# A selective-scan decoder layer: VectorE, not GpSimd, multiplies dt with the convolved input, between its products and its scans

## What is computed

```
proj = einsum('blh,he->bel', x, W_in);  hidden, gate = split(proj, 2)
hidden = silu(conv1d(hidden) + conv_bias)            # E = 1024 channels, 512 time steps
dt, Bm, Cm = split(hidden.T @ W_x, [128, 16, 16])
dts = softplus(dt @ W_dt + b_dt)                     # 1024 channels
dA  = exp(dts[..., None] * A)                        # N = 16 states for each channel
dBu = dts[..., None] * Bm * hidden[..., None]
state = dA * state + dBu                             # over the 512 time steps
y = (einsum(state, Cm) + hidden * D) * silu(gate);   out = y @ W_out
```

## Time and profile before

| | before |
|---|---|
| median of 3 runs | 1163.89 us (1163.69 to 1163.9) |
| the profiled execution: its time, and its span from first to last instruction | 1165.72 us, 1163.9 us |
| busy: VectorE, ScalarE, GpSimd, TensorE (matrix products) | 1026.1, 759.5, 748.2, 830.5 us |
| mean granted clock of TensorE | 0.874 of full speed |
| the 32 step inputs on GpSimd (L480) | 57.6 us busy |
| the dBu products on VectorE (L761, without those from `wide`) | 344.9 us busy |

### The profile page before, as it was taken

One profiled execution on the slowest core, in us unless ns is written; L12 is line 12 of the kernel. 1 busy time (PEld: TensorE's weight loads), 2 busy tenths in 40 slices (PEclk: granted clock), 3 DMA queues, 4 the chain that ended last, 5 costly groups with the idle time before them and its releaser, 6 DMA issues.

```text
span 1163.9 us, 10065 instructions
## 1 busy us (share of the span) xinstructions
PE 830.5 (71%) x2708; PEld 327.9 (28%) x2718; DVE 1026.1 (88%) x781; ACT 759.5 (65%) x1164; POOL 748.2 (64%) x419
## 2 busy tenths in 40 slices
PE   7923387877349689987459698987459657567884
PEld 2311032332024234432114233432114223222331
DVE  2569999999989998999989998899998999999833
ACT  3345567776536777786737686787655776777546
POOL 1027666667757856687766866677767867787433
PEclk9976789998679899999769899999859878787997
DMA  5174344453983343453992444344793353234000
GB/s 179 38 182 116 78 110 114 116 140 84 226 225 82 96 104 91 104 136 82 233 257 64 100 102 106 92 122 108 197 248 73 77 141 81 70 88 134 9 0 37
DMA packets 66681, 135.01 MB, mean 116 GB/s; under 512 B 13120, under 2 KB 19392, under 8 KB 66624
## 3 DMA queue, kind: packets, MB, share of 16 engines
q1 hardware_dynamic: 65904, 134.28, 45.6%
q10 hardware_dynamic: 720, 0.08, 0.0%
HBM read 62.75 MB, written 4.46 MB: 58 GB/s over the span
## 4 chain that ended last, share of the span: by engine, by line
issue 35%; DVE 28%; PE 22%; DMA 6%; ACT 5%; POOL 2%; SPq 2%; DVEq 0%; POOLq 0%; ACTq 0%
DVE st L767 19%; PE dense L866 15%; DVE dBu L761 4%; PE dense L922 3%; DMA wide<-w_out 2%; DMA Bb<-bc_rows 2%; PE dense L899 2%; DVE x L726 1%; DVE hs L745 1%; POOL st L456 1%; PE dBu L876 1%; SPq L340 1%; DVE xsc L818 1%; DVE dense L850 1%; ACT squares L592 1%
## 5 line engine op out<-in xcount | busy, mean ns | idle before, releaser
L456 POOL TENSOR_TENSOR st<-st,Cb 128x1024 f32<-128x1024 f32 x250 | 584.5, 2360 | 279.3 <-DVE dBu L761 256.0
L767 DVE TENSOR_TENSOR_SCAN st<-dA,dBu 128x1024 f32<-128x1024 f32 x256 | 570.0, 2266 | 0.0
L568 ACT ACTIVATE dA<-rep,Aneg 128x511 f32<-128x511 f32 x512 | 329.3, 710 | 119.9 <-DVE st L767 110.7
L761 DVE TENSOR_TENSOR dBu<-rep,Bb 128x1024 f32<-128x1024 f32 x250 | 344.9, 1423 | 37.9 <-DMA rep<-steps 10.9
L866 PE MATMUL dense<-xTs,Win 128*128 128x512 f32 x512 | 239.1, 611 | 14.7 <-DMA xTs<-xT 7.8
L899 PE MATMUL dense<-st,sel 128*32 128x512 f32 x1024 | 134.2, 665 | 112.8 <-POOL st L456 112.8
L866 PE MATMUL dense<-wide,hs 128*128 128x512 f32 x256 | 123.4, 640 | 37.9 <-DMA wide<-w_out 37.1
L866 PEld LDWEIGHTS dense<-xTs,Win 128*128 128x128 f32 x512 | 98.3, 196 | 147.2 <-issue 146.5
L922 PE MATMUL dense<-pj,Win 128*128 128x512 f32 (+1 forms) x192 | 94.5, 638 | 32.4 <-issue 22.2
L480 POOL TENSOR_TENSOR steps<-steps,hs 128x512 f32<-128x512 f32 x32 | 57.6, 1799 | 72.8 <-ACT steps L556 72.7
L568 ACT ACT_TABLE_LOAD x62 | 79.5, 1283 | 28.6 <-DVE st L767 24.2
(11 more groups left out here) (104 smaller groups left out, 754.6 us busy)
## 6 DMA issues: line engine op xcount, KB each, us to landing
rep<-steps SPq DMA_DIRECT2D x512, 128.0 KB, 2.4
Win<-w_in SPq DMA_DIRECT2D x64, 256.0 KB, 2.8
wide<-w_out SPq DMA_DIRECT2D x4, 2048.0 KB, 9.9
Win<-w_conv SPq DMA_DIRECT2D x24, 256.0 KB, 2.9
wide<-bc_rows SPq DMA_DIRECT2D x24, 256.0 KB, 6.5
xTs<-xT SPq DMA_DIRECT2D x4, 1024.0 KB, 7.6
Bb<-bc_rows SPq DMA_DIRECT2D x16, 256.0 KB, 7.3
Cb<-bc_rows SPq DMA_DIRECT2D x16, 256.0 KB, 5.8
```

The lines of the kernel that those rows point to most:

```text
L456: nc.gpsimd.tensor_tensor(s, s, C[:, j, :], ALU.mult).then_inc(s_p, 1)
L568: nc.scalar.activation(dA[:, u % 2, j, 1:T], rep[:, u % REPS, 0, 1:T], ACT.Exp, scale=Aneg[:, u % UNITS, j:j + 1]).then_inc(s_dA, 1)
L761: V.tensor_tensor(dBu[:, j, :], rep[:, u % REPS, 1:2, :].to_broadcast([P, JH, T]), B[:, j, :], ALU.mult).then_inc(s_mul, 1)
L767: V.tensor_tensor_scan(st[:, u % RING, j, :].rearrange("p j t -> p (j t)"), dA[:, u % 2, j, :].rearrange("p j t -> p (j t)"), dBu[:, j, :] ...
```

## The change

The multiplication leaves GpSimd's list and goes to VectorE's, as `step_inputs`. In the scan it stands inside `unit(u)`, after the two dBu products and before the two scans. `step_inputs_at(u)` names the "z" items of the step DU_LAG = 2 before the present one, so a step input that GpSimd made in unit 4 n + 3 is made by VectorE in unit 4 n + 5. The first two, before the scan, are made in their own step. VectorE also waits until the copies that read the same third of `steps` three blocks earlier have landed. GpSimd's second half of a unit now waits for the step inputs that VectorE makes in the following unit, besides the dBu products. SyncE's list, and ScalarE's and TensorE's, are as before.

```diff
+DU_LAG = 2
...
+def step_inputs_at(u):
+
+    s = UNITS + u - 1 - DU_LAG
+    return [key for key in items(*STEPS[s]) if key[0] == "z"] if u >= 1 else []
+
+
+def step_inputs_before(u):
+
+    return sum(key[0] == "z" for b, g in STEPS[:max(UNITS + u - 1 - DU_LAG, UNITS)] for key in items(b, g))
...
                 if h and u + 1 < NB * UNITS:
                     pool.wait_ge(s_mul, NH * (u + 2))
+                    pool.wait_ge(s_du, step_inputs_before(u + 2))
...
-                    n = NE * kb + i
-                    if kind == "z":
-
-                        pool.wait_ge(s_dt, n + 1)
-                        pool.wait_ge(s_hs, n + 1)
-                        nc.gpsimd.tensor_tensor(steps[:, n % 3, 1, :], steps[:, n % 3, 0, :], hs[:, kb % 2, i, :],
-                                                ALU.mult).then_inc(s_du, 1)
-                    elif kind == "qt":
+                    if kind == "qt":
...
+            def step_inputs(key):
+
+                _, b, e = key
+                n = NE * b + e
+                dve.wait_ge(s_dt, n + 1)
+                dve.wait_ge(s_hs, n + 1)
+                if n >= 3:
+                    for v in range(NQ * (n - 3), NQ * (n - 2)):
+                        dve.wait_ge(s_rep[v % REPS], 64 * (v // REPS + 1))
+                V.tensor_tensor(steps[:, n % 3, 1, :], steps[:, n % 3, 0, :], hs[:, b % 2, e, :],
+                                ALU.mult).then_inc(s_du, 1)
...
+                for key in step_inputs_at(u):
+                    step_inputs(key)
...
+                if b == -1:
+                    for key in items(b, g):
+                        if key[0] == "z":
+                            step_inputs(key)
```

## The result

The changed kernel takes 1188.16 us (median of four runs, 1183.0 to 1189.5) against 1163.89 us (four runs, 1163.69 to 1166.54): 1.0195 times as long, with a 95% interval of 1.016 to 1.023. It is slower, by 1.6 to 2.3%; 1184.0 was forecast, with a range of 1176 to 1192. The profiled execution has a span of 1185.3 us where the kernel before had 1163.9, so 21.4 us have to be found.

The account below looks back on a forecast made before the run. VectorE was taken as the main bound, with DMA binding the three later batch starts. Terms -11.7 - 6.8 + 15.3 + 23.4 = +20.2 us, added to the median 1163.89, gave 1184, range 1176 to 1192.

Parts of the forecast that it names:

- The late copy: SyncE's copies for units 32, 64, 96 go out about a unit later, delaying `Bb`: 7.07, 7.7 and 7.7 us.
- the store: Store of B and C behind that copy at units 29, 61, 93; starts 7.07 us later, 7.7 in later batches.
- the full stretch: DMA-bound time at each later batch's start, from the store of B and C; starts later, lasts as long as before.
- `w_out`: Load of `w_out` after each batch start, behind closer copies for units 36, 68, 100: 0.3 us each, 0.9 us.
- The collisions: Sixteen `dBu` pairs lengthened to 3.80 us by GpSimd's step input; eleven count, saving 11.7 us.
- The late-GpSimd places: Units 41, 57, 61, 73, 89, 93, 105, 109, where late GpSimd's product with C reaches into `dBu` pairs: 6.8 us saved.
- The product on VectorE: Step input between products and scans in units 5, 9, 13 and so on: 0.61 us, 25 count, 15.3 us added.
- the rival with 1211 us: VectorE's step input waits for GpSimd's product with C, 1.1 to 2.3 us each, 27 us more; chance 0.05.
- The six waits ahead of it: Waits ahead of VectorE's step input instruction; if not hidden, the product costs the upper end, 0.85 us.
- Unit 121's step input: Counted as covered by a following wait for TensorE of at least the product's size.
- The start: First two step inputs precede the ffn weight's quantizing, moved to about 58.9 to 67.2; cover remains, 0 us counted.
- new wait in unit 32 for the staged B: Sign of a right forecast: a short new VectorE wait there, beside the three waits for `Bb` growing to over 20 us.

Follow-up runs that it names:

- the two runs above: The changed kernel with each step input on VectorE computed twice, 1203.26 us; the changed kernel with only 8 of its 512 columns computed, 1172.93 us.

## Why the prediction was right, and where its steps were off

**The late copy: right in kind, too large by 2.3 us in 22.5.** The copies go out at unit 29's scan plus 0.11 us in all three batches, 7.0, 6.8 and 6.8 us later against VectorE; the store stands behind them; and the loss is there. From unit 29's scan to the first product with the new `Bb`, the path is 4.5 us longer in the second batch (35.31 for 30.82), 8.6 in the third (37.04 for 28.47) and 7.1 in the fourth; 7.07, 7.7 and 7.7 were forecast, 20.2 for 22.5 together.

The first error is the time from the copy to the re-reading. I had taken the 7.50 us of the second batch (284.57 to 292.07) as fixed, and added 0.8 us for the others, where it is 5.78 and 5.83. It was the other way round. With the late copy it is 5.75, 5.85 and 5.71 us (286.64 to 292.39 in the second), and so it is in the kernel before with only the wait added: 5.75, 5.88, 5.71. The 7 us belong to the second batch with the early copy (7.50 before, 7.39 with GpSimd's product cut, 6.99 one unit earlier). There the re-reading follows the store after 3.9 to 4.4 us instead of 2.7; what holds it isn't settled. In the two later batches the store had a wait of its own before (issued 3.88 us after the copy, where 3.08 is what the issuing takes). That wait is gone when the copy is late, but the store then takes 0.8 us longer to land, so nothing is added.

The rest is the full stretch itself, from the first re-reading to the landing of `Bb`: 0.8 us shorter, 1.7 longer and 0.5 longer than before. In the 21 batch starts of the seven kernels with this order it lies between 28.8 and 31.0 us, with and without the late copy, so I take these differences for scatter.

**`w_out`: too small.** I took 0.3 us a batch. Timeline of VectorE in unit 36, before and then after:

```profile
346.32 0.69 DVE L726 SCALAR_TENSOR_TENSOR x<-dense,x 128x512 f32<-128x512 f32 x1 [2.69 <-PE dense L866]
...
347.26 3.44 DVE L761 TENSOR_TENSOR dBu<-rep,Bb 128x1024 f32<-128x1024 f32 x2 [0.24 <-DVE x L726]
```

```profile
347.64 0.69 DVE L732 SCALAR_TENSOR_TENSOR x<-dense,x 128x512 f32<-128x512 f32 x1 [3.87 <-PE dense L890]
...
348.58 2.37 DVE L779 TENSOR_TENSOR dBu<-rep,Bb 128x1024 f32<-128x1024 f32 x2 [0.24 <-DVE x L732]
```

The wait for the product with `w_out` is 1.2 us longer. Its load went out at 327.97 instead of 327.23, TensorE began the product 0.9 us later (337.79 for 336.93), and the product itself took 0.5 us longer. The longer wait eats the 1.07 us that the pair behind it wins. In the three batches the wait is 1.2, 1.2 and 0.9 us longer, 2.3 us more than the forecast's 0.9. That the late copies are the cause isn't shown: the kernel before with only the late copy has a wait of 3.93 us there too, though its load is not later against VectorE, and over all ten traces these waits lie between 2.1 and 4.7 us.

**The collisions: right.** Unit 4's pair, and unit 5 with the step input, after; beside the earlier trace rows:

```profile
100.76 2.71 DVE L779 TENSOR_TENSOR dBu<-rep,Bb 128x1024 f32<-128x1024 f32 x2
...
107.76 2.75 DVE L779 TENSOR_TENSOR dBu<-rep,Bb 128x1024 f32<-128x1024 f32 x2
110.42 0.68 DVE L765 TENSOR_TENSOR steps<-steps,hs 128x512 f32<-128x512 f32 x1
111.02 4.45 DVE L787 TENSOR_TENSOR_SCAN st<-dA,dBu 128x1024 f32<-128x1024 f32 x2
```

From unit 4 on no pair of 3.8 us is left, in any of the sixteen places. From unit 5 to unit 29 the scans gained 3.24 us in 24 units, 0.54 for four (0.45 was forecast). The late-GpSimd places shrank by what the forecast gave them, 6.8 us in the eight together: unit 61's first product takes 1.6 us instead of 2.7, that of unit 109 1.2 instead of 2.8.

**The product on VectorE: right.** 0.68 to 0.69 us in the timeline, 0.60 from its start to that of the scan, where 0.61 was forecast, and the two runs above bear out its 15.3 us to within 3 us. The 0.69 us that the forecast gave from the Trainium skill, "VectorE: DVE Perf Modes", section "The TRN2 errata — SBUF-src ops pay a fixed extra latency per instruction", is the duration of the instruction, and the rows agree with it; but 0.08 us of that lies under the next instruction, so the sum goes by the 0.60. GpSimd held none of them up (the longest takes 0.69 us), so the rival with 1211 us falls. The six waits ahead of it cost nothing that shows. Unit 121's step input was counted as covered and wasn't: VectorE lost 0.6 us there.

**TensorE's stretches, not forecast.** I had left units 45 to 49 and 77 to 81 out of the sum, as ended by waits for TensorE that would be the same. They are longer: from unit 45 to unit 49 VectorE lost 2.4 us, and from 77 to 81 2.2 us. Windows of the kernel before, and then of the kernel after (columns as in the earlier trace rows, TensorE's busy time first, its granted clock third from the right):

```profile
430.00:440.00 10.00, 5.98 (x16) 2.70 (x16) 9.79 (x8) 5.57 (x10) 6.99 (x4) 0.84 0.47 111
440.00:450.00 10.00, 9.71 (x26) 4.50 (x25) 9.74 (x5) 8.04 (x11) 8.71 (x4) 0.99 0.46 121
```

```profile
430.00:440.00 10.00, 5.99 (x17) 3.19 (x16) 9.79 (x8) 5.58 (x11) 6.23 (x3) 0.76 0.36 91
440.00:450.00 10.00, 9.72 (x24) 4.38 (x23) 9.67 (x6) 7.25 (x9) 7.64 (x4) 0.90 0.37 93
```

TensorE was busy for the same time in both, but at 1.2 GHz, the lower of its two levels, for more of it (a granted clock of 0.76 and 0.90 against 0.84 and 0.99). The other traces bear this out. From unit 44's products to unit 50's, and from unit 76's to unit 82's, the mean granted clock is either 0.97 or 0.94: the twelve stretches at 0.97 take 53.5 to 53.8 us, the eight at 0.94 54.3 to 54.8. Both stretches are at 0.97 before and at 0.94 in the changed kernel. But the lower one also comes without the move (the kernel before with the late copy, second batch), and why the clock rose later is open. Against the 2.4 and 2.2 us stand about 1 us each that the shorter first product of units 45 and 77 gave back; by the scans, 1.1 and 0.9 us are lost from unit 42 to 50 and from 74 to 82.

**The start: no cost, as said.** Timeline of VectorE after, beside the earlier trace rows, and ScalarE's first activation:

```profile
55.80 0.69 DVE L765 TENSOR_TENSOR steps<-steps,hs 128x512 f32<-128x512 f32 x1 [4.69 <-ACT steps L562]
...
69.26 2.37 DVE L779 TENSOR_TENSOR dBu<-rep,Bb 128x1024 f32<-128x1024 f32 x2 [3.96 <-DMA rep<-steps]
```

```profile
69.26 6.23 ACT L574 ACTIVATE dA<-rep,Aneg 128x511 f32<-128x511 f32 x10 [0.26 <-DMA rep<-steps]
```

The quantizing moved behind the step inputs and ended at 65.3 (67.2 was forecast), 4 us before VectorE was wanted again; ScalarE had 0.26 us left, where about 1 was forecast. The cover was there, if barely. The first product is even 2.0 us earlier than before (69.26 for 71.27). How much of that is the move isn't shown: it starts between 68.36 and 71.27 in the four profiled kernels with the step input on GpSimd (69.9 on the mean), and between 66.95 and 69.26 in the six with it on VectorE (68.2).

**What I expected and didn't find.** No new wait in unit 32 for the staged B. It was copied in time (the product there starts right after the scan before it).

**The balance.** Off from the forecast were: the start -2.0, the store -2.3, `w_out` +2.3, the TensorE stretches +2.0, unit 121 +0.6, and the rest +0.6; together +1.2, which is 21.4 for 20.2. The forecast hit this closely in part by luck, because its errors had both signs. The other 3 us between 1184.0 and the median of 1188.16 come from which executions were profiled: before, the profiled one took 1165.72 us, 1.8 over the median, and after 1187.18, 1.0 under it. Of the three other times after, two are near 1189 and one is 1183.0, with a mean granted clock of TensorE of 0.869 where the others have 0.858 or 0.859. That the clock makes this spread is argued, not shown. The stated range was no plain sum of its terms either: their upper ends add up to 12.8 us, so 1197 and not 1192.

## What to carry to other kernels

When work moves from one engine to another, look at who reads its result, and above all whether a queue that takes its entries in order waits for it: here a copy that was itself not urgent stood ahead of a store that was, and one unit of delay cost 21 us in a change whose own work about paid for itself. The same move one unit earlier is a gain of 0.4%. And in a stretch that DMA bounds, moving the first transfer forward gives only what the transfers put behind it don't take again.

## What the runs showed of the hardware

- Two VectorE instructions of 0.68 and 0.69 us with two inputs in SBUF start 0.72 us apart when the second waits for the first, while the scan behind them starts 0.61 us after the second. The waiting costs 0.1 us here, not the 0.24 us of idle time in the earlier trace rows.
- The meetings of VectorE and GpSimd cost both: a pair of 3.80 us is one of 2.73 us when GpSimd's product has 8 columns, and the GpSimd product takes 2.25 us beside a `dBu` product and 1.27 us alone. The Trainium skill, "SBUF — State Buffer", section "SBUF: two separate sides", says that of two such instructions the one that starts first blocks the other whole. The trace of the kernel before agrees: in that pair GpSimd's product ends at 104.67, 1.1 us after VectorE's first product (103.54), and VectorE's second ends 1.1 us after that (105.76).
- A store of 64 KB to DRAM that is waited for took 1.7 us from its issue to that of the re-reading where it stood ahead of the copies (552.38 to 554.07), 2.7 us just behind the copies and a weight load (289.72 to 292.39), and 4.4 us in the second batch of the kernel before, behind the same transfers (287.65 to 292.07). What makes the last two differ isn't settled.
- The DMA engines move much the same in a full stretch in all versions (231 to 251 GB/s, from 1 us after the first re-reading to 1 us before the product that needs `Bb`), and it takes 28.8 to 31.0 us from the first re-reading to the last of `Bb` when the copies and the weight load are ahead of the store, 32.3 to 33.9 when they come after the re-reading.
- GpSimd's first product with C waits for `Cb`, until 80.89 us after and 81.63 before. The scan that began 2.0 us earlier thus had GpSimd's backlog beside more of its products: the pairs of units 2 and 3 take 9.6 us together after (5.06 and 4.58) and 8.8 before (6.10 and 2.72).
